# The output projection's bias: from two products of ones to one VectorE addition

## The reference, cut to what matters

```
x = x + _layernorm(_L0_attn_ref(_layernorm(x), ...))       # stage A
x = x + _layernorm(_L0_ffn_ref(_layernorm(x), ...))        # stage B
x = x + _layernorm(_L1_attn_ref(_layernorm(x), Wq, Wkv, Wo, bo))
x = x + _layernorm(_L1_ffn_ref(_layernorm(x), ...))

def _L1_attn_ref(x, Wq, Wkv, Wo, bo):     # 2048 tokens, 1024 wide
    ...
    return jnp.dot(ctx, Wo) + bo          # ctx: result of the attention
```

## Time and profile before

| | us |
|---|---|
| median of 3 runs | 2226.28 (2221.66 to 2226.42) |
| the profiled execution's own time | 2220.29 |
| its span, first to last instruction | 2218.1 |
| PE busy in the span | 2043.4 (92%) |
| DVE busy | 1452.8 (65%) |
| POOL busy | 997.4 (45%) |
| ACT busy | 939.9 (42%) |

### The profile page before, as it was taken

One profiled execution on the slowest core, in us unless ns is written; L12 is line 12 of the kernel. 1 busy time (PEld: TensorE's weight loads), 2 busy tenths in 40 slices (PEclk: granted clock), 3 DMA queues, 4 the chain that ended last, 5 costly groups with the idle time before them and its releaser, 6 DMA issues.

```text
span 2218.1 us, 31076 instructions
## 1 busy us (share of the span) xinstructions
PE 2043.4 (92%) x10632; PEld 1490.1 (67%) x10632; DVE 1452.8 (65%) x3351; ACT 939.9 (42%) x1959; POOL 997.4 (45%) x866
## 2 busy tenths in 40 slices
PE   4788877899999989989999999899988999999998
PEld 4545436788888879755556555555554688888887
DVE  7987788677777763287665667577668555544533
ACT  4755664222333323135554555455556333322311
POOL 1344677444444420017885586667883233120000
PEclk9999998999999999999999999999998999999999
DMA  5221266122111247522224722322224465544432
GB/s 181 76 103 42 84 226 238 38 77 77 66 70 68 74 166 269 130 54 54 69 67 103 208 71 75 81 70 73 59 68 121 134 229 175 165 155 144 133 117 92
DMA packets 148028, 249.79 MB, mean 113 GB/s; under 512 B 27150, under 2 KB 79246, under 8 KB 147648
## 3 DMA queue, kind: packets, MB, share of 16 engines
q1 hardware_dynamic: 136864, 227.89, 32.7%
q10 hardware_dynamic: 11008, 19.93, 2.8%
HBM read 140.01 MB, written 76.02 MB: 97 GB/s over the span
## 4 chain that ended last, share of the span: by engine, by line
PE 55%; POOL 13%; DVE 9%; issue 5%; ACT 2%; DMA 1%; SPq 1%; ACTq 1%; POOLq 0%; DVEq 0%
POOL c_S L2405 8%; PE PS L2595 4%; PE PS L2596 4%; PE PS L2599 4%; PE PS L1113 3%; PE PS L1114 3%; PE PS L1115 3%; PE PS L1973 3%; PE PS L1955 2%; PE PS L1988 2%; PE PS L1146 2%; PE PS L1148 2%; PE PS L1147 2%; DVE PS L2297 2%; PE PS L1931 2%
## 5 line engine op out<-in xcount | busy, mean ns | idle before, releaser
L2142 ACT ACTIVATE c_P<-PS 128x512 f32<-128x512 f32 (+3 forms) x768 | 356.9, 494 | 319.0 <-PE PS L1973 299.2
L1955 PE MATMUL PS<-c_K,c_Q 96*128 96x512 f32 (+3 forms) x768 | 276.5, 370 | 21.1 <-DVE cst L2297 14.0
L1973 PE MATMUL PS<-c_Q,c_K 97*128 97x512 f32 (+3 forms) x768 | 280.1, 378 | 7.2 <-DMA c_Q<-c_mT 3.9
L2405 POOL TENSOR_TENSOR c_S<-c_S,c_P 128x2048 f32<-128x2048 f32 (+3 forms) x94 | 272.7, 2901 | 8.5
L1973 PEld LDWEIGHTS PS<-c_Q,c_K 97*128 97x128 f32 x768 | 146.2, 193 | 172.6 <-ACT c_P L2142 97.7
L2293 DVE TENSOR_REDUCE cst<-PS 128x1 f32<-128x512 f32 x256 | 176.1, 688 | 91.9 <-PE PS L1955 91.3
L1955 PEld LDWEIGHTS PS<-c_K,c_Q 96*128 96x128 f32 x768 | 149.6, 195 | 77.5 <-DVE cst L2297 38.3
L1988 PE MATMUL PS<-c_P,c_V 128*32 128x512 f32 (+3 forms) x1536 | 166.3, 505 | 16.3 <-ACT c_P L2142 10.7
L2297 DVE CUSTOM_DVE_ANT_0 PS<-PS,maskw,cst 128x128 f32<-128x128 f32 (+3 forms) x256 | 142.9, 558 | 58.6 <-PE PS L1955 42.2
L199 POOL TENSOR_TENSOR maskw<-maskw,mhalf 128x1 f32<-128x1 f32 x64 | 37.1, 580 | 305.2 <-DVE maskw L168 304.9
L1246 ACT ACTIVATE b_g<-PS 128x460 f32<-128x460 f32 x96 | 53.0, 552 | 274.8 <-PE PS L1120 273.9
(11 more groups left out here) (298 smaller groups left out, 4953.5 us busy)
## 6 DMA issues: line engine op xcount, KB each, us to landing
a_xin<-in_x SPq DMA_DIRECT2D x32, 512.0 KB, 4.3
d_x<-scr SPq DMA_DIRECT2D x32, 512.0 KB, 4.8
c_Q<-c_qh SPq DMA_DIRECT2D x240, 64.0 KB, 2.0
scr<-a_xin SPq DMA_DIRECT2D x16, 512.0 KB, 6.1
b_xn<-scr SPq DMA_DIRECT2D x16, 512.0 KB, 5.6
b_x<-scr SPq DMA_DIRECT2D x16, 512.0 KB, 4.7
scr<-b_x SPq DMA_DIRECT2D x16, 512.0 KB, 2.6
scr<-b_y SPq DMA_DIRECT2D x16, 512.0 KB, 3.0
```

The costliest lines, as they stand in the source:

```text
L1955: e.matmul(bank[:, 0:hi - lo], self.Q4[0:96, 4 * (o % 3) + g, 128 * t:128 * t + 128], self.K4[0:96, HEADS[o % 8], lo:hi], start=True, stop ...
L1973: e.matmul(self.k.bank(i % 3)[:, 0:hi - lo], self.K4[0:97, HEADS[o % 8], 128 * kt:128 * kt + 128], self.Q4[0:97, 4 * (o % 3) + g, lo:hi], ...
L2142: e.activation(self.P[:, R % 3, g, 0:hi - lo], self.k.bank(i % 3)[:, 0:hi - lo], ACT.Exp, scale=SCALE).then_inc(self.exp_s.s, 1)
L2405: e.tensor_tensor(S[:, :, 512 - n:512], S[:, :, 512 - n:512], P[:, :, 0:n], ADD).then_inc(self.psum_s.s, 1)
```

## The change

`load_bias` and its wait go, in stage D only. `d_bo` becomes a full tile of 128 equal rows, loaded by one DMA (512 KB in place of 256 KB), and the two matmuls of ones go from tiles 0 to 15. In their place DVE adds `d_bo` to the 128x1024 sum in PSUM, before it takes the statistics, and waits for its own addition. PE's wait and SP's wait for the bias go. `sb("gap", ...)` holds the place of the ones in memory, so that nothing behind it moves.

```
-            self.bo, self.one = sb("bo", [128, 1024], F32R), sb("one", [128, 128], F32R)
+            self.bo = sb("bo", [128, 1024])
+            sb("gap", [128, 128])
...
-        e.dma_start(self.org[0:64, :], self.k.io["bo"].partition_broadcast(64)).then_inc(self.ldb.s, 16)
+        e.dma_start(self.bo[:, :], self.k.io["bo"].partition_broadcast(128)).then_inc(self.ldb.s, 16)
...
-                e.wait_ge(*self.bias(1))                       # in sp, u == 1
                 self.sp_org(e, 0)
...
-        if half == 1 and u == 0:                               # in pe_out
-            e.wait_ge(*self.bias(1))
...
-                m = e.matmul(o, l, wh[:, c, cols], start=False, stop=c == 7 and u >= NT)
-        if half == 1 and u < NT:
-            for s in range(2):
-                m = e.matmul(k.bank(2 * (u % 2) + s), self.one[:, :], self.bo[:, 512 * s:512 * s + 512], start=False, stop=True)
+                m = e.matmul(o, l, wh[:, c, cols], start=False, stop=c == 7)
         m.then_inc(self.out.s, 1)
...
-        load_bias(e, self.k.mine["dve"].on(e), self.bo, self.one, self.org, self.ldb(1), self.bias)
...
                 e.wait_ge(*self.out(2 * u))                    # in dve
-                T.dve_y(e, own, t, k.bank(2 * ((u - 1) % 2), 2))
+                y = k.bank(2 * ((u - 1) % 2), 2)
+                if u == 1:
+                    e.wait_ge(*self.ldb(1))
+                if u <= NT:
+                    e.tensor_tensor(y, y, self.bo[:, :], ADD).then_inc(self.biased.s, 1)
+                    e.wait_ge(*self.biased(u))
+                T.dve_y(e, own, t, y)
                 T.dve_y_nm(e, t)
```

More of the change, by code:

```diff
@@ L2455, in __init__ @@
         self.ldb, self.ldd, self.ldo, self.ldu = (Sig(k, "d_ld" + n, 16) for n in "bdou")
-        self.bias, self.whi, self.wlo, self.xhi, self.xlo, self.out, self.sums, self.acc_s = k.sigs(
-            "d_", "bias whi wlo xhi xlo out sums acc")
+        self.biased, self.whi, self.wlo, self.xhi, self.xlo, self.out, self.sums, self.acc_s = k.sigs(
+            "d_", "biased whi wlo xhi xlo out sums acc")
         self.lo2 = Sig(k, "d_lo2")
```

## The result

| | before | changed |
|---|---|---|
| median, us | 2226.28 (2221.66 to 2230.04, 13 runs) | 2232.8 (2228.54 to 2238.06, 13 runs) |
| ratio to before, 95% interval | | 1.0026 (1.0019 to 1.0034) |
| span of the profiled execution, us | 2218.1 | 2226.3 |
| first matmul of tile 0, us in the span | 1734.36 | 1734.98 |
| from there to the end of the span (stage D), us | 483.74 | 491.32 |

The changed kernel is slower by 0.26%, which is 5.8 us by the ratio (4.2 to 7.6 by its interval); 4.2 us were forecast. The median of 2232.8 lies 0.1 us above the forecast's own range (2229.3 to 2232.7). The profiled execution shows 8.2 us, of which 7.6 lie in stage D.

A forecast was written before the change was run, and what follows sets the result against it. PE bounded turns 1 to 4, with 0.77 us of slack in the DVE, ACT and POOL loop. Chunk (12,0) 5.8 us late, less 1.8, plus 0.2: 4.2 us slower, median 2230.5, range 2220 to 2236 (forecast alone 2229.3 to 2232.7).

The forecast's parts named there:

- What bounds: Stage D before: PE sets the pace in turns 1 to 4 at 11.33 us, beside a DVE, ACT and POOL loop of 10.56.
- The round trip: Stage D's closed loop of DVE, ACT and POOL: 10.56 us in turns 1 to 4, 12.10 in turns 5 to 8 before.
- the 0.23 at POOL: L168 to L176, turns 5 to 8 before: 0.23 us lost as L199 queues behind the accumulator; the addition hides it.
- PE's first stall: Turns 1 to 8: PE may lead by 2.5 us, used up by 0.94 us a turn, later 2.25; stalls from tile 5 or 6.
- Part 1: PE, tiles 0 to 15: each removed pair of products of ones saves 0.45 us of work, 7.25 us for 16 pairs.
- Part 2: DVE, 16 additions in the round trip: 1.26 us each (1.22 plus 0.03 to 0.04 of wait), bounds 1.14 and 1.48.
- Part 3: Turns 1 to 8: 11.82 us each in turns 1 to 4, 13.13 in 5 to 8; accumulator for (9,0) 5.7 us late.
- Part 4: Turns 9 to 15: chunk (12,0) starts 5.8 us later, tiles 12 to 15 give 1.8 back, 0.2 for longer waits.
- Part 5: The dropped `load_bias`, the larger `bo` load and SP's missing wait: no gain, up to 1 us if the cover were thinner.
- Rival 2: TensorE's clock falls at new waits, counting in full at (12,0): 1.7 us more, 5.9 slower, up to 8, 2232.5; chance 0.19.
- Rival 1: Stage D: PE stays the bound and the addition hides beside it; 7.25 us gain, 2219.0 us; chance 0.14.
- rival 3: Part of the loss is covered (DVE earlier out of stage C, more overlap): 1 to 2 us slower, about 2227.8; chance 0.11.

The follow-up runs named there:

- e1: The changed kernel without the addition, so neither products of ones nor addition; stage D 481.27 us, ratio 0.9999 to the kernel before.
- e2: The changed kernel plus two more 512-column matmuls in tiles 0 to 15 in place of the products of ones; stage D 493.93 us, ratio 1.0053 to before.
- e3: The changed kernel with the addition over only the first 512 of 1024 columns; stage D 484.42 us, ratio 1.0013 to the kernel before.
- e6: The kernel before with the up weights in turns 5, 6, 9 and 10 in place of 5 to 8; stage D 480.92 us, ratio 0.9983.
- e7: The kernel before with products of ones for tiles 0 to 11 and the addition only for tiles 12 to 15; stage D 481.86 us, ratio 0.9995.
- e4: The changed kernel with 12 useless matmuls ahead of PE's wait at (9,0); stage D 490.94 us, ratio 1.0033 to the kernel before.
- e5: The changed kernel with 12 useless matmuls ahead of each PE wait, at (9,0) and (12,0); stage D 489.37 us, ratio 1.0029 to the kernel before.

## Why the prediction was right, and which terms were off

- What bounds: right. The round trip became the bound in turns 1 to 4, and e1, e2 and e3 show that it is the addition in it and not PE's work that sets the time there. Its slack was less than the 0.77 us of the prediction: e6 shows the free round trip at 10.97 us, so 10.74 without the 0.23 at POOL and not 10.56. That is 0.59 us of slack, and 10.74 + 1.26 gives the 12.00 of turn 4.
- PE's first stall was forecast for tile 5 or 6 and came at tile 4. The prediction's own numbers say so: 2.5 us of room and 0.94 us a turn are used up in turn 3, in which tile 4 starts.
- Part 1, 0.45 us for a pair: right where PE is the bound: tiles 12 to 15 give 1.7 us here and 1.8 in e7, for 4 x 0.45 = 1.8.
- Part 2, the price of 1.26 us: right. Neither bound was approached. The statistics behind the addition start 0.04 us after its end, where an instruction without such a wait starts some 0.08 before it. The Trainium skill ("VectorE: DVE Perf Modes", section "The DRAIN you can't avoid") says that the semaphore costs nothing extra; here it costs about 0.12 us. The addition with one source and its result in PSUM has a median of 1220 ns, L2769 with neither 1.22 us. The Trainium skill (same page, section "The TRN2 errata") gives a PSUM source more cycles than one in SBUF; these rows show no such difference.
- Part 3, to (9,0): the term was 5.7 us and measured 7.5. Turns 5 to 8 are right (13.14 for 13.13). Turns 1 to 4 were forecast at 11.82 each and took 12.93, 12.21, 11.92 and 12.00, 1.8 us more in all. The step that failed is that a turn was priced from rows of quiet turns; 0.1 to 0.2 us of each turn is the slack that was counted too large. In turn 1 DVE's addition to `d_x` now runs into POOL's last multiplication of stage C, in DVE's and POOL's timelines:

```profile
1753.99 2.19 DVE L183 TENSOR_TENSOR d_x<-d_x,d_y 128x1024 f32<-128x1024 f32 x1 [1.27 <-ACT d_y L215]
```

```profile
1753.81 1.29 POOL L2362 TENSOR_TENSOR c_cH<-c_cH,c_cS 128x512 f32<-128x512 f32 x1 [1.29 <-DMA c_cS<-rec_d]
```

  It takes 2.19 us and not 1.23. In e3 DVE's timeline has the same addition 0.32 us ahead of the multiplication, and the pair the other way round: the addition keeps 1.23 us, the multiplication takes 2.06 in place of 1.29, and the `d_xl` that starts beside it takes 1.78 in place of 0.69:

```profile
1758.63 1.23 DVE L183 TENSOR_TENSOR d_x<-d_x,d_y 128x1024 f32<-128x1024 f32 x1 [1.27 <-ACT d_y L215]
1759.77 1.78 DVE L2729 TENSOR_TENSOR d_xl<-d_in,d_xh 128x512 fp32r<-128x512 f32 x1
```

```profile
1758.95 2.06 POOL L2362 TENSOR_TENSOR c_cH<-c_cH,c_cS 128x512 f32<-128x512 f32 x1 [1.78 <-DMA c_cS<-rec_d]
```

  So in both kernels it is the one that starts second that takes longer than it does alone. In turn 2 the second half's `d_xl` takes 1.10 us, beside a copy of POOL's, and in turns 3 to 9 0.82 to 0.83, where it had 0.69 to 0.73 in turns 1 to 5 before. A kernel without the multiplication at that place was not tried.
- Part 4, to the chunk (12,0): the term was 0.1 us and measured 1.8. The wait and the stall are there, at the places forecast (2.39 us at (9,0), 1.39 at (12,0), where the sum had PE ready 5.25 - 2 x 0.45 = 4.35 us late and the chunk 5.83, so 1.5 us apart). What was missing is that the fall of the clock behind (9,0), 1.7 us before, was 3.3 here. e4 takes all 3.3 away from PE, and e4's second fall and the wait for DVE leave a gain of 0.4 in the stage.
- Part 5, at nothing: nothing speaks against it. Tile 0 starts at 1734.98 us in place of 1734.36, inside the spread of that start between executions.
- Rival 2 had the right mechanism at the wrong place: the 1.39 us at (12,0) left the clock at 1.00, and the price came at (9,0), where I had counted it as unchanged. In e4 the place was right too, since the wait there had grown to 2.36 us. That the median (2232.8) is so near to its 2232.5 is in part luck: its sum has the clock but not the 1.8 us of turns 1 to 4.
- Rival 1 is refuted by the result, which is slower, and by e2; rival 3 by the first cut: nothing came back.
- The median moved by 6.5 us, the ratio says 5.8, stage D of the profiled execution 7.6, the forecast 4.2. The two missed terms (1.8 and 1.7) add to 3.5, the whole of the 3.4 between the forecast and stage D. Both point the same way, so no error covered another, and stage D of this execution lies above the forecast's own 3.0 to 6.4. Why the timed runs show less is open; a fall of the clock that is short in some executions, as in e3, would do it, but only one execution of each kernel has a trace.

## What to carry to other kernels

An engine that is busy for all of a stretch may still lead its neighbours' round trip by a few per cent only; the slack is near to the wait in brackets of the instructions that close the loop (0.59 to 0.67 us here, for a measured 0.59), and work moved off the busy engine is worth no more than that slack, while work put into the loop is paid in all that exceeds it. Where a turn shows the loop without the busy engine, as in e6, take it from there. The same operation was free in another part of the same loop (e7): look for turns in which the busy engine has extra work. A wait of PE is priced with what the clock does behind it, and filling one wait helped little where the next one on the same chain grew and the clock fell behind that (e4); filling both kept it up (e5).

## What the runs showed of the hardware

- A wait of 1.39 us on PE with full work on both sides left the granted clock at 1.00, and so did the nine waits for `d_xl` of 0.47 to 1.17 us (1.00 from 1780 to 1848); one of 2.36 us let it fall (0.72 over 6 us). At (9,0), with 16 thin matmuls of 128x1 behind it, a wait of 1.09 us was followed by a fall; without any wait (e6) the thin ones did nothing.
- The fall behind (9,0) came in two sizes. From the thin matmuls to the first chunk, (11,1), before and e7 take 34.85 and 34.87 us where e6 has 33.16, so 1.7 more; e2, with as many matmuls, takes 36.47, so 3.3 more. Without the pairs e4 has 31.79: e3 is 1.7 above it, the changed kernel and e1 3.3. The wait was 2.39 to 2.43 us in the changed kernel, e1, e2 and e3 alike, so the size isn't given by the wait alone. What sets it stays open.
- Where DVE's addition to `d_x` and POOL's multiplication ran at the same time, the second to start took 2.19 us for 1.23 (DVE) or 2.06 for 1.29 (POOL). The addition with a source in PSUM kept 1.21 to 1.23 us in all its 16 places, also beside POOL's accumulation.
- Tile 0 started up to 8 us apart in the profiles, behind stages with the same code but for the last instructions; that is as much as the whole effect. The cuts of the profile at fixed instructions repeat within 0.2 us where the code of the stretch and the clock are the same (117.58, 117.74 and 117.71 us to (9,0)), while the timed ratios of e5 and e7 could not tell 2 us from nothing.
